# A four-layer graph network on one core: one-hot products for the first two chunks of layers 1 to 3

## What is computed

```python
h = x @ enc_node_w + enc_node_b
e = edge_attr @ enc_edge_w + enc_edge_b
for layer in range(4):                       # z = relu(layernorm(h)) from layer 1 on
    msg = relu(z[src] + e) + 1e-7            # one row of 64 per edge
    m = msg * t
    ex = exp(m - segment_max(m, dst)[dst])   # softmax over the edges of a node
    agg = segment_sum(msg * ex / segment_sum(ex, dst)[dst], dst)
    out = z + agg
    conv = relu(layernorm(out @ w1 + b1)) @ w2 + b2
    h = conv if layer == 0 else h + conv
return layernorm(x + relu(layernorm(h)))
```

## Time and profile before

| | |
|---|---|
| median of the runs | 3496.52 us |
| the profiled execution | 3510.39 us |
| its span, first to last instruction | 3508.6 us |
| VectorE (DVE) busy | 2860.7 us, 82% |
| TensorE (PE) busy | 2678.7 us, 76% |
| GpSimd (POOL) busy | 2403.4 us, 68% |
| ScalarE (ACT) busy | 1772.0 us, 51% |
| granted TensorE clock, mean | 0.855 |

### The profile page before, as it was taken

One profiled execution on the slowest core, in us unless ns is written; L12 is line 12 of the kernel. 1 busy time (PEld: TensorE's weight loads), 2 busy tenths in 40 slices (PEclk: granted clock), 3 DMA queues, 4 the chain that ended last, 5 costly groups with the idle time before them and its releaser, 6 DMA issues.

```text
span 3508.6 us, 49979 instructions
## 1 busy us (share of the span) xinstructions
PE 2678.7 (76%) x19276; PEld 1382.1 (39%) x19276; DVE 2860.7 (82%) x2825; ACT 1772.0 (51%) x2228; POOL 2403.4 (68%) x2477
## 2 busy tenths in 40 slices
PE   3677677777438989998754999989943889998964
PEld 2333333333224444444332444444422444444433
DVE  6899999999757787888865888888885689887985
ACT  2676775665424454445433444454542445444544
POOL 5777777777457776777547777777745777776752
PEclk6888788898559999999856999999965999999985
DMA  5999999999548999999736999999954899999971
GB/s 147 275 285 292 287 279 258 291 277 273 116 133 236 275 287 285 296 284 283 186 77 175 286 296 290 286 290 296 254 116 135 232 280 295 292 295 272 288 184 40
DMA packets 1048367, 853.28 MB, mean 243 GB/s; under 512 B 912955, under 2 KB 938560, under 8 KB 1018369
## 3 DMA queue, kind: packets, MB, share of 16 engines
q1 hardware_dynamic: 940688, 470.61, 53.7%
q10 hardware_dynamic: 27232, 285.62, 21.7%
q0 software_dynamic: 80208, 93.86, 10.5%
HBM read 537.69 MB, written 312.14 MB: 242 GB/s over the span
## 4 chain that ended last, share of the span: by engine, by line
PE 26%; DVE 26%; POOL 16%; SPq 11%; issue 9%; ACT 7%; DMA 6%; POOLq 0%; DVEq 0%; ACTq 0%
PE X L546 20%; POOL gath L486 14%; SPq L356 6%; DVE decay L905 6%; DVE state_all L936 5%; DMA keep<-keep_dram 4%; SPq L346 4%; DVE rows_all L891 4%; PE X L527 3%; DVE X L910 3%; DVE one_hot L1000 3%; ACT X L658 2%; ACT msg L656 2%; DVE state_all L920 2%; PE X L556 1%
## 5 line engine op out<-in xcount | busy, mean ns | idle before, releaser
L486 POOL DMA_INDIRECT gath<-z_table,idx x2344 | 2283.2, 974 | 894.8 <-issue 716.1
L546 PE MATMUL X<-one_hot,z_parts 128*64 128x512 fp8e5 x10200 | 1173.0, 391 | 93.0 <-DVE one_hot L1000 93.0
L546 PEld LDWEIGHTS X<-one_hot,z_parts 128*64 128x64 bf16 x10200 | 580.7, 113 | 734.9 <-issue 135.2
L546 PE MATMUL X<-between,z_parts 128*64 128x512 fp8e5 x6300 | 700.2, 381 | 0.0
L527 PE MATMUL X<-attr,enc_edge 128*128 128x512 f32 x824 | 490.6, 725 | 240.8 <-DVE state_all L936 233.5
L668 ACT ACTIVATE decay<-X 128x1024 f32<-128x1024 f32 (+2 forms) x216 | 209.1, 968 | 907.8 <-DVE X L910 796.4
L891 DVE STREAM_TRANSPOSE rows_all<-state_all 128x1024 f32<-128x1024 f32 (+3 forms) x432 | 505.7, 1171 | 7.5
L546 PEld LDWEIGHTS X<-between,z_parts 128*64 128x64 bf16 x6300 | 352.3, 111 | 369.7 <-issue 62.2
L920 DVE TENSOR_TENSOR_SCAN state_all<-decay,state_all,X 128x1024 f32<-128x1024 f32 (+2 forms) x216 | 468.1, 2167 | 20.0 <-ACT X L673 20.0
L905 DVE TENSOR_TENSOR_SCAN decay<-X,decay 128x1023 f32<-128x1023 f32 (+2 forms) x216 | 477.1, 2209 | 7.9 <-DVE decay L903 0.2
L936 DVE TENSOR_TENSOR_SCAN state_all<-decay,state_all,X 128x1024 f32<-128x1024 f32 (+2 forms) x216 | 467.8, 2166 | 0.0
(11 more groups left out here) (160 smaller groups left out, 1549.3 us busy)
## 6 DMA issues: line engine op xcount, KB each, us to landing
rows_table<-rows_all SPq DMA_DIRECT2D x784, 256.0 KB
attr<-attr_t SPq DMA_DIRECT2D x196, 512.0 KB
one_hot<-one_hot_dram ACTq DMA_DIRECT2D x45, 1920.0 KB
between<-one_hot_dram ACTq DMA_DIRECT2D x42, 1920.0 KB
one_hot<-one_hot_dram ACTq DMA_DIRECT2D x45, 1280.0 KB
one_hot_dram<-one_hot SPq DMA_DIRECT2D x29, 1920.0 KB
between<-one_hot_dram ACTq DMA_DIRECT2D x42, 1280.0 KB
gath<-z_table,idx POOLq DMA_INDIRECT x2344
```

Source lines behind the costliest of these rows:

```text
L486: pool.indirect_dma_start(out=gath[s][:, n * F:(n + 1) * F], out_offset=None, in_=z_table, in_offset=bass.IndirectOffsetOnAxis(ap=idx[:, c ...
L546: last = nc.tensor.matmul(x[h * F:(h + 1) * F, BANK:CH], z_parts[:, i * GB + k, third, :], bank[:, i, k, h * BANK:(h + 1) * BANK], start=F ...
```

## The change

In layers 1 to 3 chunks 0 and 1 are chosen too, so there are 31 banks in place of 29. In layer 0 these two stay as they were: their banks are built in the slots of chunks 50 and 52, which had no build. On TensorE, `add_by_one_hot` for chunk 0 stands behind the first two edge products, that of chunk 1 behind `add_rows` of chunk 0 and the edge product of chunk 2. GpSimd issues 6 gathers for chunk 0 in place of 14, and 8 for chunk 1 in place of 16. The bank of chunk 0 is loaded in the layer before: for layer 1 at the end of layer 0, ahead of the node stage, for layers 2 and 3 behind the messages of chunk 50. The bank of chunk 1 is loaded at the layer's start, behind the wait for `z_split` and ahead of the messages of chunk 0; those of chunks 4 and 5 behind the messages of chunks 0 and 1. The tables for the banks grow from 232 to 248 columns.

```diff
@@ -54,8 +54,10 @@
 HOT_SLOTS = 2
 BIT_SLOTS = 3
 FIRST_CHOSEN = [c for c in range(NCH) if c % 2 == 0 and 4 <= c <= 48]
-CHOSEN = [c for c in range(NCH) if (c % 2 == 0 or c % 8 == 5) and 4 <= c <= 48]
-BANKS = sorted(set(FIRST_CHOSEN + CHOSEN))
+CHOSEN = [c for c in range(NCH) if c < 2 or (c % 2 == 0 or c % 8 == 5) and 4 <= c <= 48]
+BUILD_SLOT = {0: 50, 1: 52}
+BANKS = sorted(set(FIRST_CHOSEN + CHOSEN), key=lambda c: BUILD_SLOT.get(c, c))
+BANK_SLOTS = [BUILD_SLOT.get(c, c) for c in BANKS]
 NB1H = len(BANKS)
 PART_SCALE = [2.0 ** 14, 2.0 ** 13, 2.0 ** 11, 2.0 ** 7, 2.0 ** -1]
 BANK_COLS = HALVES * BANK
@@ -81,7 +83,11 @@
 
 
 def bank_of(c):
-    return BANKS.index(c) if c in BANKS else None
+    return BANKS.index(c)
+
+
+def bank_built_for(slot):
+    return BANK_SLOTS.index(slot) if slot in BANK_SLOTS else None
 
 
 def pieces_before(layer, c):
@@ -116,7 +122,7 @@
     GATHERS_UP_TO.append((GATHERS_UP_TO[_g - SLOTS] if _g >= SLOTS else 0) + HALVES * (gathered_tiles(_g // NCH, _c) - first_tile(_c)))
 
 assert sum(WIDTHS) == COLS and NCH % SLOTS == 0 and NCH % 2 == 0 and NT % GB == 0 and SUB * P == NB1H * BANK_COLS
-assert all(tiles(c) == KT and c >= 4 for c in BANKS)
+assert all(tiles(c) == KT for c in BANKS) and min(BANK_SLOTS) >= 4 and SKIP < BANK // P
 
 
 def gnn_kernel(nc, x_nodes, x_t, dst_stream, src_tiles, src_banks, attr_t, enc_node_w, enc_node_b, enc_edge_w, enc_edge_b,
@@ -416,10 +422,10 @@
                         loaded += 1
                     if layer == 0:
                         for part in (1, 0):
-                            n = bank_of(c + 2 + (part == 0))
+                            n = bank_built_for(c + 2 + (part == 0))
                             if n is not None:
                                 store_part(n, part)
-                        n = bank_of(c + 2)
+                        n = bank_built_for(c + 2)
                         if n is not None and n + BIT_SLOTS < NB1H:
                             load_bits(n + BIT_SLOTS)
                     if layer == LAYERS - 1 and c == 0:
@@ -597,10 +603,15 @@
                     pe.wait_ge(h_added, layer * NG)
                 edge_product(layer, 0)
                 edge_product(layer, 1)
+                if 0 in chosen(layer):
+                    add_by_one_hot(layer, 0, 0)
+                    add_by_one_hot(layer, 0, 1)
                 for c in range(NCH):
                     add_rows(layer, c)
                     if c + 2 < NCH:
                         edge_product(layer, c + 2)
+                    if c == 0 and 1 in chosen(layer):
+                        add_by_one_hot(layer, 1, 0)
                     if c + 1 in chosen(layer):
                         add_by_one_hot(layer, c + 1, 1)
                     if c + 2 in chosen(layer):
@@ -762,17 +773,22 @@
                         penalties(layer, 0)
                         if layer == 0:
                             act.wait_ge(t_landed, 16)
+                        else:
+                            for part in range(len(PARTS)):
+                                load_part(layer, 1, part)
                     messages(layer, c)
                     if layer > 0:
-                        if c == 0:
-                            for j in range(HOT_SLOTS):
-                                for part in range(len(PARTS)):
-                                    load_part(layer, j, part)
                         for part in range(len(PARTS)):
-                            j = CHOSEN.index(c + 1 - part) + HOT_SLOTS if c + 1 - part in CHOSEN else len(CHOSEN)
-                            if j < len(CHOSEN):
-                                load_part(layer, j, part)
-                    n = bank_of(c + 3)
+                            k = c if part == 1 or c == 0 else c + 1
+                            if k in CHOSEN and k != 1 and CHOSEN.index(k) + HOT_SLOTS < len(CHOSEN):
+                                load_part(layer, CHOSEN.index(k) + HOT_SLOTS, part)
+                        if c == 1:
+                            for part in range(len(PARTS)):
+                                load_part(layer, CHOSEN.index(1) + HOT_SLOTS, part)
+                        if c == CHOSEN[-1] + 2 and layer < LAYERS - 1:
+                            for part in range(len(PARTS)):
+                                load_part(layer + 1, 0, part)
+                    n = bank_built_for(c + 3)
                     building = layer == 0 and n is not None
                     if building:
                         spread_lanes(n, range(0, 2))
@@ -796,6 +812,8 @@
                                   rows[g % 2][a * SQ:(a + 1) * SQ, 0:n].rearrange("i b q j -> i b (q j)")).then_inc(stored[g % 2], 16)
                 nc.scalar.activation(sd3[0][:, 0:1], eps_col[:, :], ACT.Sqrt)
                 if layer == 0:
+                    for part in range(len(PARTS)):
+                        load_part(1, 0, part)
                     act.wait_ge(params_landed, 16 * N_PARAM)
                 denominators(layer, 0)
                 for i in range(NG + 3):
@@ -1138,10 +1156,10 @@
                 for c in range(NCH):
                     softmax_sums(layer, c)
                     if layer == 0:
-                        if bank_of(c + 2) is not None:
-                            build_part(bank_of(c + 2), 1)
-                        if bank_of(c + 3) is not None:
-                            build_part(bank_of(c + 3), 0)
+                        if bank_built_for(c + 2) is not None:
+                            build_part(bank_built_for(c + 2), 1)
+                        if bank_built_for(c + 3) is not None:
+                            build_part(bank_built_for(c + 3), 0)
                         if c == PREP_CHUNKS[-1] + 1:
                             find_positions()
                             centre_weights()
```

## The result

Before 3499.5 us (median of four runs), after 3462.4 us (four runs); ratio of the runs 0.9898, 95% interval 0.9874 to 0.9921, so 36 us or 1.0% faster. Forecast were -30 us and 3466. A repetition on another chip of the same speed gave 0.9901 (0.9883 to 0.9919). On one slower chip, where the kernel before takes 4531 us, the change gains nothing (first experiment).

The account below looks back on a forecast made before the run. It took layer 0 as bound by DVE and the start of layers 1 to 3 by waiting for gathers; -57 (starts) + 20 (layer 0) + 7 (layer ends) = -30 us, 3466 on the median, range 3442 to 3495.

Parts of the forecast that it names:

- The start: Start of layers 1 to 3: sixteen gathers fewer end the wait 20 us sooner; 19 us gained per layer, 57 in three.
- the two chains meet: Start of layer 1: PE's product chain allows chunk 5's edge product at 1053.5, chunk 3's gathers at 1052.6, nearly together.
- The 1 us for crowding among DMAs: Start of layers 1 to 3: bank loads fit with little air beside other DMA work; 1 us charged, bounds 0 and 10.
- The middle: Layers 1 to 3 behind the start: all engines are coupled, so their distances in time were taken as kept.
- The clock: Chunk 0's added products on PE: about 4 us at the low level, half lost, so 18.3 us; bounds 16.3 and 32.6.
- Rival 2: PE stays at the low clock through both added banks: slower, +63 us, 3560, chance 0.06; smaller form 3503, 0.04.
- Layer 0: Layer 0's end: builds 14.2, stores 2, larger position tables 0.5, load ahead of the node stage 3; together 20 us lost.
- The layers' ends: Ends of layers 1 and 2: bank 0's load finds too little free DMA, 3.6 us late, twice; 7 us lost (0 to 16).
- signs of being wrong: Listed trace signs, among them PE waiting for bank 1 and keep loads holding ACT over 5 us in chunks 50 to 53.
- Rival 1: Layers 1 to 3: DMA is the bound and eats half of the start's gain; 3495, chance 0.15.
- rival 3: The start gains its full 20.4 us per layer, and loads and stores find room: -46 us, 3450, chance 0.20.
- Rival 4: Middle of layers 1 to 3: fewer gathers buy only slack, so only costs stay, +27 us, 3523, chance 0.02.

Follow-up runs that it names:

- first experiment: The changed kernel run again on the slow chip, against the kernel before (4530.7 us there): ratio 1.0018.
- e1b: Kernel before with second halves of chunks 0 and 1 left out in layers 1 to 3, neither gathered nor given products: 0.9833 of the kernel before, -58.5 us.
- e7: Changed kernel with bank 0's loads moved, plus 12 dummy products keeping PE busy before the split of z: 0.9878 of the kernel before, beside 0.9872 without them.
- e6: Changed kernel with bank 0's loads moved, plus a third added bank, for chunk 2 (32 banks): 1.013 of the kernel before.
- e2: Kernel before plus only layer 0's part, the two extra banks built and stored but not loaded or used: 1.0041 of the kernel before, +14.3 us.
- r0b: The changed kernel run again, unaltered, on a chip as fast as the first: 0.9901 of the kernel before.
- e5: Changed kernel with bank 0's loads moved and only chunk 1's bank added (30 banks): 0.9932 of the kernel before.

## Why the prediction was right

**The start.** The step was 20 us a layer less 1: chunk 4 moved by 19.7, 20.8 and 19.7 us against the split of z. Its parts came as worked out: 18.6 us for chunk 0's products (18.3), x of chunk 1 at 1048.6, 37.9 behind the end of the split at 1010.7 (37.6), the run's end 77.9 behind it (77.3). That the two chains meet is shown from three sides: no products at all change nothing (e1b), shorter ones change under 1 us (e7), a third bank of them makes the start 7 us later (e6). The 1 us for crowding among DMAs can't be told apart.

**The middle.** The forecast took all distances behind the start as kept. From DVE's chunk 4 to its chunk 47 the three layers take 1842.5 us in sum before, and 1830.0 in e2, where they do the same work; in the changed kernel 1829.9 and, in r0b, 1838.1. So no change is seen there beside what two executions of the same layers differ by.

**The clock.** About four us at the low level and then the high one is what the stretches show, 0.50 for 3.2 us, a mean of 0.83 over the next 4 and 1.00 from 1018 on. The Trainium skill ("TensorE: Matmul & The Clock Gate", section "What's actually happening") has activity release the half-rate clock; the trace agrees. Rival 2 is ruled out on the first chip. On the second its form comes about, products late in the chain, but through missing instructions and not by the clock alone: chunk 0's products take 43.6 us there, more than the 32.6 that the low level throughout would make (the mean clock of the run is 0.81 there, 0.88 here).

**Layer 0.** 20 us forecast, 16.4 in the trace: 12.7 in the chunks and 3.7 for the load ahead of the node stage (3 forecast). For the builds alone e2 gives 13 in its trace and 14.3 by its ratio (14.2 + 0.5 forecast); nothing is seen for the stores (2 forecast).

**The layers' ends.** 7 us forecast, 5.8 and 6.2 us in the traces, from chunk 47's begin to the first node gather (5.9 and 5.9 in r0b): this term was too small by 5 us. I had counted the free share of DMA. What costs is SP's queue: the stores are slow to issue beside the load. DVE waits 4.4 us for one of them to land, and the keep load behind them holds ACT for 7.9 us, so that DVE waits once more. The keep load ends last; by these rows a prompt one alone would have given back some 1.3 us (DVE waits 2.12 us for ACT, 0.81 before), and the rest is the store's. Such a hold of ACT for over 5 us was named among the signs of being wrong, and it came. The trace of before had the slow issue already, not at a layer's end but in the middle of layer 1, where a bank load is issued at 1135.48:

```profile
1134.18 8.95 SPq L356 DMA_DIRECT2D rows_table<-rows_all  x4
```

The rule of the Trainium skill ("DMA: Bandwidth & Descriptors", section "Issuing engines are not separate DMA queues"), that what several engines issue runs on the same DMA engines and interleaves, agrees with transfers that delay each other; of the 8.2 us that the forecast drew from it for each end, some 6 came.

**Sum.** With the measured terms: -60 + 14.3 + 3.7 + 12.0 = -30; measured -36 with an interval of -28 to -44. That this is the forecast's own -30 is partly luck: the start gave 3 us more, layer 0 cost 2 less, and the layers' ends took 5 more. The runs agree among themselves: builds +14.3 and fewer gathers -58.5 make -44 (each known to some 5 to 8 us), and the kernel with moved loads has -45 and -47. So against the gathers' whole value the added products and DMAs cost, beside the builds, only the 11 us of the misplaced loads. Rival 1 (DMA eats half) falls by this; rival 3's mechanism, room for everything, is nearly what moving the loads gives. Rival 4 falls by e1b and e5. One slip: the chances given for rivals 2 and 4 make 0.12, not 0.11.

## What to carry to other kernels

When an engine waits at the start of a stage for one resource, move work there from it to an engine that idles, but only until the two chains meet: with one bank more the start was 7 us later again. Place a prefetch by the queue that it slows, not by the free share of DMA: ask what is issued beside it, what is due behind that in the same queue, and what the issuing engine itself must wait for first. And a gain that comes from loading a nearly full engine may be gone on a chip where that engine is slower.

## What was not expected of the hardware

The kernel before took 4531 us on one chip and some 3500 on the others. In the changed kernel's traces VectorE's and GpSimd's instructions have the same durations on both (the scan of L923 2209 ns, a gather 970 and 974 ns), and PE's one-hot products come 1.4 us and more apart. Four row stores of 256 KB took SP 4.0 us to issue alone and 10.6 to 11.5 us beside a bank load issued by ACT. The loads from a bits table of 32 banks took a median of 18.3 us to land instead of 13.6 with 31 and 14.5 with 29, and their 1024-byte packets 123.5 ns instead of 52.8 and 52.2.
